# M kept in DRAM between the sequences, and Ln and Exp in place of a reciprocal

## What is computed

```python
def attn_a(x):                       # softmax over keys, one head of width 1024
    q, k, v = split(x @ w_qkv.T)
    probs = softmax(q @ k.T / 8)
    out = probs @ v
    out = swapaxes(out, 1, 2).reshape(out.shape)
    return out @ w_proj.T + b_proj

def attn_b(x):                       # groups of 4 positions, 8 heads of 128
    qk_in, v_in = x @ proj_qk_w.T + b, x @ proj_v_w.T + b
    q, k, v = qk_in @ wq.T, qk_in @ wk.T, v_in @ wv.T
    scores = where(diag, min, q @ k.T / sqrt(128))
    return softmax(scores) @ v @ out_proj_w.T + out_proj_b

def ffn(x):
    return (silu(x @ wg.T) * (x @ wu.T)) @ wd.T

x = x + attn_a(layernorm(x)); x = x + ffn(layernorm(x))
x = x + attn_b(layernorm(x)); x = x + ffn(layernorm(x))
```

## Time and profile before

| what | value |
|---|---|
| median of 2 runs | 5630.09 us (5567.73 and 5692.46) |
| profiled execution | 5056.83 us, slowest core's span 5055.3 us |
| spans of the 8 cores | 5024.1 to 5055.3 us |
| mean granted TensorE clock | 0.866 to 0.871 |
| busy on the slowest core | TensorE 4006.1 us (79%), VectorE 1121.0 (22%), ScalarE 977.0 (19%), POOL 183.8 (4%) |
| transfers | 160.57 MB, mean 32 GB/s |

### The profile page before, as it was taken

The page is one execution under the profiler, slowest core; times in us unless marked ns, Lnnn a source line. Parts: engine busy times, 40 slices in busy tenths (PEclk is TensorE's granted clock), DMA queues, the critical chain, the costliest instruction groups (busy, mean ns, idle before and its releaser), DMA issues.

```text
span 5055.3 us, 48902 instructions; the slowest of 8 cores (5024.1 to 5055.3 us)
## 1 busy us (share of the span) xinstructions
PE 4006.1 (79%) x17856; PEld 1692.1 (33%) x17856; DVE 1121.0 (22%) x1616; ACT 977.0 (19%) x1472; POOL 183.8 (4%) x338
## 2 busy tenths in 40 slices
PE   3899968999385555599974999859998566559999
PEld 1233323444132222144431333314443222213444
DVE  1200032211013444321103100132112333442211
ACT  0331222110032221311001321131101222222110
POOL 0000000000000000000000000000000000000000
PEclk8789978999697777699986899969998777769999
DMA  6001012222610000022343001102224000002223
GB/s 125 1 1 14 5 17 30 40 39 36 100 51 0 1 0 9 3 41 40 63 111 79 1 1 17 17 9 38 38 36 90 0 1 0 2 7 36 40 46 89
DMA packets 67860, 160.57 MB, mean 32 GB/s; under 512 B 6064, under 2 KB 6192, under 8 KB 63536
## 3 DMA queue, kind: packets, MB, share of 16 engines
q0 software_dynamic: 62816, 123.82, 16.0%
q1 hardware_dynamic: 4816, 33.63, 1.8%
HBM read 245.55 MB, written 23.09 MB: 53 GB/s over the span
## 4 chain that ended last, share of the span: by engine, by line
PE 77%; DVE 10%; ACT 6%; issue 3%; another core or an unknown queue 2%; DMA 2%; ACTq 0%; DVEq 0%; POOLq 0%; POOL 0%
PE PS L95 52%; PE PS L663 13%; PE PS L500 5%; DVE PS L950 4%; PE PS L541 2%; PE PS L267 2%; ACT SQ L261 2%; PE PS L340 1%; DVE XN L234 1%; DVE XN L287 1%; DMA AR<-wb 1%; DVE WB L966 1%; ACT WB L957 1%; PE PS L975 1%
## 5 line engine op out<-in xcount | busy, mean ns | idle before, releaser
L95 PE MATMUL PS<-XN,WB 128*128 128x512 bf16 x6144 | 1363.2, 385 | 65.7 <-DVE XN L287 62.9
L95 PEld LDWEIGHTS PS<-XN,WB 128*128 128x128 bf16 x6144 | 607.3, 99 | 821.9 <-issue 121.9
L663 PE MATMUL PS<-AR,WB 128*128 128x512 bf16 x3072 | 663.7, 379 | 4.5 <-DVE AR L612 4.5
L612 DVE SCALAR_TENSOR_TENSOR AR<-PS,SQ 128x512 bf16<-128x512 f32 x384 | 265.7, 692 | 1117.5 <-PE PS L95 1077.0
L95 PE MATMUL PS<-AR,XN 128*128 128x512 bf16 x1792 | 431.6, 393 | 2.0 <-ACT AR L450 1.8
L606 ACT ACTIVATE SQ<-PS 128x512 bf16<-128x512 f32 x384 | 229.6, 598 | 1046.0 <-PE PS L95 1045.9
L663 PEld LDWEIGHTS PS<-AR,WB 128*128 128x128 bf16 x3072 | 300.3, 98 | 367.9 <-issue 6.3
L95 PE MATMUL PS<-AR 128*128 128x512 bf16 x1408 | 362.4, 419 | 14.5 <-DVE AR L287 11.7
L95 PE MATMUL PS<-XN,AR 128*128 128x512 bf16 x1280 | 320.6, 412 | 15.4 <-DVE XN L287 9.7
L500 PE MATMUL PS<-AR 128*128 128x512 bf16 x1024 | 246.5, 385 | 19.8 <-DVE MISC L511 15.8
L950 DVE RECIPROCAL PS<-PS 1x1024 f32<-1x1024 f32 x32 | 209.7, 6553 | 204.9 <-PE PS L939 204.9
(11 more groups left out here) (91 smaller groups left out, 2004.3 us busy)
## 6 DMA issues: line engine op xcount, KB each, us to landing
WB<-wg POOLq DMA_DIRECT2D x96, 256.0 KB, 4.0
WB<-wu POOLq DMA_DIRECT2D x96, 256.0 KB, 4.8
WB<-wdc POOLq DMA_DIRECT2D x96, 256.0 KB, 4.9
XF<-x SPq DMA_DIRECT2D x2, 8192.0 KB, 43.7
y<-XF SPq DMA_DIRECT2D x16, 1024.0 KB, 8.1
AR<-wb POOLq DMA_DIRECT2D x5, 2048.0 KB, 49.4
AR<-wqk POOLq DMA_DIRECT2D x2, 4096.0 KB, 58.4
WB<-wpc POOLq DMA_DIRECT2D x32, 256.0 KB, 4.0
```

The costliest lines, as they stand in the source:

```text
L95: (lambda e: e.matmul(_o, _l, _r, start=_st, stop=_sp)))(),
L612: (lambda e: e.scalar_tensor_tensor(ar(S * _c + TT * _g, TT), bank(_bu), DEQ, _h, ALU.mult, ALU.mult)))(),
L663: (lambda e: e.matmul(bank(_b), wbs(_sl, 128 * (_c % 8), 128), ar(S * _c + TT * _g, TT), start=(_c == 0), stop=(_c == HHC - 1))))(),
```

## The change

It has two parts, put in together.

The first is in the M stage. In sequence 0 the wqk load becomes two, chunks 0 to 3 into slots 0 to 3 and chunks 4 to 7 into slots 4 to 7. The first matmul of a wave waits for the first load, the first matmul of chunk 4 for the second. After the last wave M is stored from AR to a new DRAM tensor d_fm by a transfer on POOL's queue, which waits for the last M cast; the load of wvT comes behind it in the same queue. In sequence 1 the wqk load, the waves and their casts aren't issued; M is loaded from d_fm (2 MB of bfloat16), and the first two layer norms follow each other.

The second is in b_tail. VectorE's reciprocal of the row of sums becomes ScalarE's Ln, from banks 2 and 3 into banks 4 and 5, and ScalarE's copy becomes Exp with scale -1, so exp(-ln s) stands for 1/s. The waits stay as they are, apart from the semaphore that the first of the pair raises.

```diff
--- before.py
+++ after.py
@@ -147,6 +147,7 @@
     d_wbn1 = nc.dram_tensor("wbn1", [CH, 128, 1024], F32, kind="ExternalInput").ap()
     d_fw = nc.dram_tensor("fw", [3, CH, 128, 1024], BF16).ap()
     d_fb = nc.dram_tensor("fb", [128, 40], F32).ap()
+    d_fm = nc.dram_tensor("fm", [128, 8192], BF16).ap()
     d_misc = nc.dram_tensor("misc", [128, 58], F32, kind="ExternalInput").ap()
     d_cbf = nc.dram_tensor("cbf", [128, 256], F32, kind="ExternalInput").ap()
     d_y = nc.dram_tensor("y", [NSEQ, CH, 128, S], F32, kind="ExternalOutput").ap()
@@ -323,12 +324,6 @@
             groups = [(ec, eh) for ec in range(CH) for eh in range(2)]
             waves = [groups[0:6], groups[6:12], groups[12:16]]
 
-            wqld = dma(sch, "gpsimd",
-                       lambda e: e.dma_start(
-                           out=bass.AP(AR, 0, [[24 * S, 128], [2048, CH], [1, 2048]]),
-                           in_=d_wqk.rearrange("c w p e -> p c w e")),
-                       wkeys=[("ar", s_) for s_ in range(8)])
-
             def emit_mwave(wave):
                 bank_w = {gi: sch.wqw(("ps", gi)) for gi in range(len(wave))}
                 for oc in range(CH):
@@ -342,7 +337,8 @@
                                          ar(2048 * _oc + 128 * _ec, 128),
                                          ar(2048 * _oc + 1024 + 512 * _eh, 512),
                                          start=_st, stop=_sp)))(),
-                                    waits=(([wqld] if gi == 0 and oc == 0 else []) +
+                                    waits=(([wqld_a if oc < 4 else wqld_b]
+                                            if gi == 0 and oc in (0, 4) else []) +
                                            (bank_w[gi] if oc == 0 else [])),
                                     inc=("t" if gi == len(wave) - 1 else None))
                 for gi, (ec, eh) in enumerate(wave):
@@ -381,13 +377,32 @@
                            wkeys=arslot(V_B + 1024 * (4 * tg + tt) + 512 * h2, 512),
                            waits=[gm], inc="s")
 
-            emit_mwave(waves[0])
-            emit_ln1(0)
-            emit_mwave(waves[1])
-            emit_ln1(1)
-            emit_mwave(waves[2])
             if s_i == 0:
+                wqld_a = dma(sch, "gpsimd",
+                             lambda e: e.dma_start(
+                                 out=bass.AP(AR, 0, [[24 * S, 128], [2048, 4], [1, 2048]]),
+                                 in_=d_wqk[0:4].rearrange("c w p e -> p c w e")),
+                             wkeys=[("ar", s_) for s_ in range(4)])
+                wqld_b = dma(sch, "gpsimd",
+                             lambda e: e.dma_start(
+                                 out=bass.AP(AR, 8192, [[24 * S, 128], [2048, 4], [1, 2048]]),
+                                 in_=d_wqk[4:8].rearrange("c w p e -> p c w e")),
+                             wkeys=[("ar", s_) for s_ in range(4, 8)])
+                emit_mwave(waves[0])
+                emit_ln1(0)
+                emit_mwave(waves[1])
+                emit_ln1(1)
+                emit_mwave(waves[2])
+                dma(sch, "gpsimd",
+                    lambda e: e.dma_start(out=d_fm, in_=AR[:, M_B:M_B + 8192]),
+                    rkeys=arslot(M_B, 8192), waits=[("v", sch.cnt["v"])])
                 tap("m", AR[:, M_B:M_B + 8192])
+            else:
+                dma(sch, "gpsimd",
+                    lambda e: e.dma_start(out=AR[:, M_B:M_B + 8192], in_=d_fm),
+                    wkeys=arslot(M_B, 8192))
+                emit_ln1(0)
+                emit_ln1(1)
             wvld = dma(sch, "gpsimd",
                        lambda e: e.dma_start(
                            out=bass.AP(AR, WVT_B, [[24 * S, 128], [1024, CH], [1, 1024]]),
@@ -946,16 +961,17 @@
                 sch.wrote(("ps", 2), smw)
                 sch.wrote(("ps", 3), smw)
                 sch.read(("wb", 1), smw)
-                rc0 = ev(sch, "vector",
-                         lambda e: e.reciprocal(PS[0:1, 2048:3072],
-                                                PS[0:1, 1024:2048]),
+                rc0 = ev(sch, "scalar",
+                         lambda e: e.activation(PS[0:1, 2048:3072],
+                                                PS[0:1, 1024:2048], AF.Ln),
                          rbanks=[2, 3], wkeys=[("psrow45",)], waits=[smw] +
-                         sch.wqw(("ps", 4)) + sch.wqw(("ps", 5)), inc="v")
+                         sch.wqw(("ps", 4)) + sch.wqw(("ps", 5)), inc="s")
                 sch.wrote(("ps", 4), rc0)
                 sch.wrote(("ps", 5), rc0)
                 rcm = ev(sch, "scalar",
                          lambda e: e.activation(WB[0:1, 2048:3072],
-                                                PS[0:1, 2048:3072], AF.Copy),
+                                                PS[0:1, 2048:3072], AF.Exp,
+                                                scale=-1.0),
                          rbanks=[4, 5], wkeys=[("wb", 2)], waits=[rc0], inc="s")
                 mm_group(sch, [(PS[:, 1024:1536], ones_row, WB[0:1, 2048:2560])],
                          banks=[2], reads=[("wb", 2)], waits=[rcm])
```

## The result

| | before | after |
|---|---|---|
| median of all executions, side by side | 5463.42 us (5033.94 to 5692.46, 10 executions) | 4807.96 us (4801.46 to 5396.65, 11) |
| profiled execution | 5056.83 us | 4806.38 us |
| core spans in it | 5024.1 to 5055.3 us | 4791.0 to 4804.8 us |
| mean granted clock | 0.866 to 0.871 | 0.882 to 0.884 |

The ratio is 0.9542, with a 95% interval of 0.9526 to 0.9558: faster by 4.6%. In some executions of either kernel the cores of one die or both run at a lower granted clock and take some per cent longer; the two runs of before that were known at the prediction (5567.73 and 5692.46) were of that kind, and the ratio is taken without such executions.

The account below looks back on a forecast made before the run. The prediction took TensorE's matmul chain as the bound, with time to be had only where TensorE waits. 177 + 29 + 48 + 6 - 6 = 254 us off the 5630.1 us median gave 5376 us, range 5275 to 5475.

Parts of the forecast that it names:

- the base: Whole kernel: savings summed against the profiled 5056.8 us, then the same microseconds taken off the two-run median, 5630.1 us.
- The reciprocal: In each of 32 tails, Ln at 1.01 us replaces the 6.55 us reciprocal, all exposed; 177 us saved.
- Rival 3: Tails: Ln and Exp don't share a table, two loads of 1283 ns per tail; 5458 us, chance 0.05.
- The clock in the tails: Dense 16-matmul groups behind 24 tails run faster after shorter waits, 1.2 us per group; 29 us saved.
- the bound of 64: Groups behind 24 tails: all the lost clock comes back, 24 x 2.68 = 64 us.
- will mostly fall again: TensorE's clock in a new tail, about 8 us of small work and short waits, mostly falls but returns sooner.
- Rival 1: Tails: the clock comes back fully; 289 us saved, 5341 us, chance 0.10.
- The second sequence: Second sequence's start: wqk load and M waves go, M is loaded instead; V projection 48 us sooner, bounds 40 and 54.
- the landing of x: Second sequence: x lands 36 us after its issue instead of 44.8, at 2670, bounds 2664 and 2678.
- The first sequence: First sequence's start: wqk halves gain 6 us, a new wait for wvT costs 6 us, and the two cancel.
- Rival 2: Transfers gain nothing: x lands as before, halves bring nothing, wvT wait is 16 us; 5400 us, chance 0.08.
- Rival 4: Feed-forward stages: dense pace falls one more step, 9216 matmuls at 49 ns more; 5828 us, chance 0.03.

Follow-up runs that it names:

- wvT ahead of the store of M: Changed kernel with the first sequence's wvT load issued before the M waves, so ahead of the store of M; core span 4780 us.
- the second part alone: Kernel before with only Ln and Exp in the 32 tails, M still computed in both sequences; ratio 0.9644, core span 4830 us.
- Ln twice: Changed kernel with the Ln of each tail issued a second time as a repeat; core span 4821 us.
- Fillers in before: Kernel before, reciprocal kept, with 7, 37 and 6 matmuls that nobody reads in each tail's three TensorE waits; core span 4957 us.
- fillers in after: Changed kernel with 7, 11 and 6 matmuls that nobody reads in each tail's three TensorE waits; ratio 0.9424, core span 4724 us.
- one wqk load again: Changed kernel with the wqk load in one piece instead of two; ratio 0.9532, core span 4789 us.

## Why the prediction was wrong, and where it was right

**What failed is the base, in the step "So I sum against 5056.8 and subtract the same microseconds from 5630.1".** It rests on the estimate that the timed runs had the lower pace in the dense stages and that the next ones would have it too. The saving was summed against the profiled execution, 5056.8 to 4803, and the profiled execution of after came out at 4806.4. The saving was then taken off the median, 5630.1 - 254 = 5376, and the range of 5275 to 5475 laid around that; the median of after was 4808. The median of two was no property of the kernel: beside after, three executions of before took 5034 to 5038 us and six of after 4801 to 4808, and the dense stretch of 1424 matmuls takes 307.52 us in both kernels. The pace that was guessed does occur: core 1 of the profiled execution of "wvT ahead of the store of M", with a span of 4960 us, has 1440 dense matmuls in 379.87 us, 264 ns each, in its first feed-forward stretch, and 216 ns in the later ones. What was wrong is to take it for what the next measurement would have. What could be seen: the profiled execution of before has its dense stretches at 216 ns, so the 573 us on top of 5057 belonged to two executions, which a further measurement need not repeat. With its own sums the range should have reached from 5056.8 - 301 = 4756 to 5630.1 - 180 = 5450.

**The ratio fits by luck.** The forecast as a ratio was 5376 / 5630 = 0.955, and 0.9542 was measured. The saving was put 23 us too high, a tenth, and the base 12% too high, and the two errors cancel. The same 254 us against 5056.8 give 0.950.

**The reciprocal: right.** Forecast 177 us; the waits before the broadcasts shrank by 183.0 (by 183.3 with the second part alone). Ln takes 0.979 us where I took 1.01. Of the 183, 32 x (6.553 - 0.979) = 178.4 are the instruction itself; the other 0.14 us per tail lie in the hops, which I had left as they were. The run with Ln twice shows that the wait is exposed in full. Rival 3 fell: no load in the tails. The Trainium skill, page ScalarE: Activation LUTs, section Table sets, has Exp and Ln in one set, and the trace agrees, with 15 loads at this line of the layer norms before and after.

**The clock in the tails: mechanism right, size wrong.** I had taken "a bit under half of the bound", 29 of 64 us. Fillers in before give 63 and fillers in after still 65, so hardly anything came back; the change had about 7 of it (190 - 183). That the bound of 64 meets the 63 is luck. It was 24 times the excess of the one group shown, 6.14 us, and that is one of the longest: the 23 groups behind tails that the timeline of core 6 of before prints as 16 matmuls take 4.53 to 6.03 us, 5.47 in the mean (5.65 on core 1). Against 3.62 that is 44 to 49 us for 24 groups, and the rest of the 63 is in the small matmuls, which the bound left out. In after the mean of 20 such groups is 5.33, 0.1 to 0.3 us less per tail, and the 64 broadcasts take 26.8 us instead of 32.2: 9 to 13 us, near the 7 of the remainder. The argument "will mostly fall again" was right, "and come back sooner" was worth a few tenths of a microsecond per tail. Rival 1, all of it back, is refuted.

**The second sequence: 41, not 48.** Removing the waves is worth what was said, and M's load is hidden: nobody waited for it. The term that was mis-sized is the landing of x. I put it 36 us after its issue, and it was 43.1, because the load of wvT, which goes out 14 us ahead of it, ran beside it until 2548.5. Nor did I see that the same loads slow the last store of y (12.5 us; 3.9 with them held). x lands as late after the down projection as before, for which I had given 40 us as the lower bound. The layer norms behind it came as forecast: 2563.78 to 2625.16 is 61.4 us, forecast 62.5.

**The first sequence: right in sum.** +6 and -6 were forecast; +5 for the halves by the trace (one load again) and a wait of 6.8 to 8.2 us for wvT (forecast 2 to 9) were found. V1 starts at 160.8 to 164.9 in the profiled execution of after and at 159.0 to 161.8 when measured again; in before it is 158.9 to 161.8 on six of the eight cores. So nothing is gained or lost. The 160.5 that I named fits by chance: it was taken from the 166.46 of core 1, which had 265 ns matmuls there, and so was the pace behind the 6 us. Rival 2, transfers gain nothing, holds in one of its pieces only, x's landing.

**Not in the sum:** on core 6 of after, the slowest, the first matmul from fw in the second attention B waits 8.82 us for its 6 MB load, which took 28.6 us; on the other seven nobody waits for it. The 3 us between 93.1 with the second part alone and 89.9 in after aren't that wait: both kernels have cores with 1077.7 and with 1081.1 us there.

**The account:** 183 (waits) + 7 (clock) + 41 (second start) + 0 (first) = 231 us, against 177 + 29 + 48 + 0 = 254. The 7 is itself the remainder of one run (190 - 183), so that the sum comes out to the microsecond says less than it seems. Rival 4, a slower dense pace, was not seen: the feed-forward stretches after take 307.52 to 307.68 us for 1424 matmuls.

## What to carry to other kernels

Where two runs and a profile of the same kernel differ by 10%, sum against the fastest execution, forecast a ratio, and let the range in absolute time reach over both bases. An operation on one row of PSUM that stands between two matmuls cost its full length in each of the 32 tails, so choose the engine by its measured duration for that shape; here the waits went, but the clock did not come back until TensorE's remaining short waits were filled with work. A bound is taken from the mean of all groups and not from the one that is shown (5.5 us against 6.14). A load that nobody waits for still costs if it is issued beside one that somebody waits for: look at the order within a queue (wvT behind the store of M, 7 to 9 us) and at what shares the DMA engines (x, 27 us).

## What the runs showed of the hardware

- VectorE's reciprocal of 1x1024 float32 in PSUM takes 6553 ns, ScalarE's Ln of the same row 979 ns and Exp to bfloat16 1013 ns.
- In the small work of a tail, with three waits of 1.5 to 2.5 us, TensorE's granted clock falls to 1.2 GHz (0.50 from 1528 to 1532 in after), and shortening the longest wait from 8.2 to 2.5 us brings only about 7 of some 65 us back. Filling all three waits with matmuls keeps it near 2.4 GHz: 16 matmuls take 3.62 us instead of 5.3 to 5.7 in the mean.
- An 8 MB load on SyncE's queue takes 43.1 us while loads of 2 and 4 MB from POOL's queue run, and 25.4 us alone, that is 8.39 MB / 25.4 us = 330 GB/s. While x is under way in after all 16 engines are busy and move 187 to 292 GB/s, wvT's load among them until 2548.5 (stretches of after, core 6: PE to POOL busy, clock, DMA share, GB/s):

```profile
2520.00:2530.00 10.00, 0.00 (x0) 0.00 (x0) 0.00 (x0) 0.00 (x0) 0.00 (x0) 0.50 1.05 187
...
2550.00:2560.00 10.00, 0.00 (x0) 0.00 (x0) 0.00 (x0) 0.00 (x0) 0.00 (x0) 0.50 1.02 292
```

The Trainium skill, page DMA: Bandwidth & Descriptors, section Issuing engines are not separate DMA queues, says that transfers interleave on the same engines whoever starts them; the runs agree and put 17.7 us on it for x (43.1 against 25.4).
